# Fourier neural operator with a transformer block: spectra stored as (ky, kx, image), and one eviction of the spectral products moved to VectorE

## What is computed

```python
def _spectral_conv(h, w1, w2):
    xf = jnp.fft.rfft2(h)
    top = jnp.einsum('bixy,ioxy->boxy', xf[:, :, :M1, :M2], w1)
    bot = jnp.einsum('bixy,ioxy->boxy', xf[:, :, -M1:, :M2], w2)
    of = jnp.zeros(xf.shape, dtype=xf.dtype)
    of = of.at[:, :, :M1, :M2].set(top)
    of = of.at[:, :, -M1:, :M2].set(bot)
    return jnp.fft.irfft2(of, s=(h.shape[-2], h.shape[-1]))
for l in range(LAYERS):
    sc = _spectral_conv(h, w1r[l] + 1j * w1i[l], w2r[l] + 1j * w2i[l])
    pw = jnp.einsum('bihw,oi->bohw', h, pw_w[l]) + pw_b[l][None, :, None, None]
    y = sc + pw
    mean = y.mean(axis=(0, 2, 3), keepdims=True)
    var = y.var(axis=(0, 2, 3), keepdims=True)
    y = (y - mean) * jax.lax.rsqrt(var + EPS)
    y = y * gamma[l][None, :, None, None] + beta[l][None, :, None, None]
    h = jax.nn.gelu(y, approximate=False)
```

## Time and profile before

| | |
|---|---|
| Runs | 2538.08, 2528.74 and 2523.18 us, median 2528.74 |
| Profiled execution | 2528.25 us, of it the span 2526.5 us |
| Busy in the span | TensorE 2173.5 us (86%), VectorE 1648.5 (65%), ScalarE 1669.2 (66%), GpSimd 152.0 (6%) |
| Granted TensorE clock | 0.937 of full speed on average |
| HBM traffic | 203 GB/s over the span |
| Spectral products | four stages, of which layer 0's lies at 75.5 to 127.7 us and layer 1's at 532.5 to 584.9 us |

### The profile page before, as it was taken

How to read it: one execution, slowest core, us unless ns; L and a number is a source line. 1 busy time by engine, 2 the same in 40 slices (tenths; PEclk the granted TensorE clock), 3 DMA queues, 4 the chain that set the end, 5 groups by cost and what they waited for, 6 DMA issues and landing times. The chain is left out here.

```text
span 2526.5 us, 79368 instructions
## 1 busy us (share of the span) xinstructions
PE 2173.5 (86%) x34571; PEld 1449.5 (57%) x34571; DVE 1648.5 (65%) x2562; ACT 1669.2 (66%) x2640; POOL 152.0 (6%) x172
## 2 busy tenths in 40 slices
PE   6769979976997998599979967995999599964999
PEld 4657757765665776566657765664222355552444
DVE  3868878874777887577778874775000677754444
ACT  1924468876776887777778885675999466641333
POOL 0000000000000000000000000000000022202443
PEclk9989989988998999899989988998999699976999
DMA  5655567758997774899977659997652100012433
GB/s 184 227 169 203 185 255 260 240 177 274 343 349 283 265 262 151 276 329 331 323 269 257 217 201 302 360 370 274 218 178 88 37 2 2 2 29 55 105 87 71
DMA packets 174006, 518.62 MB, mean 205 GB/s; under 512 B 22687, under 2 KB 37759, under 8 KB 173439
## 3 DMA queue, kind: packets, MB, share of 16 engines
q1 hardware_dynamic: 173663, 513.55, 60.6%
HBM read 343.73 MB, written 170.37 MB: 203 GB/s over the span
## 5 line engine op out<-in xcount | busy, mean ns | idle before, releaser
L426 PE MATMUL P<-cst,mem 128*128 128x128 f32 (+1 forms) x3760 | 500.9, 282 | 54.2 <-DMA mem<-in_x 14.5
L426 PEld LDWEIGHTS P<-cst,mem 128*128 128x128 f32 (+1 forms) x3760 | 414.7, 143 | 162.2 <-issue 129.8
L685 ACT ACTIVATE mem<-P,small 128x512 f32<-128x512 f32 x512 | 310.6, 688 | 287.3 <-PE P L534 263.6
L844 DVE BATCH_NORM_STATS2 mem<-mem 128x6 f32<-128x512 f32 x512 | 315.2, 678 | 4.8 <-ACT mem L685 4.8
L882 DVE COPY mem<-P 128x512 f32<-128x512 f32 x384 | 247.9, 687 | 99.6 <-PE P L426 98.5
L534 PEld LDWEIGHTS P<-cst,mem 64*128 64x128 f32 (+1 forms) x5120 | 240.5, 166 | 100.7 <-issue 100.3
L534 PE MATMUL P<-cst,mem 64*128 64x128 f32 (+1 forms) x5120 | 262.6, 275 | 3.8 <-issue 3.5
L675 ACT ACTIVATE mem<-mem,small 128x1024 f32<-128x1024 f32 x192 | 229.2, 1250 | 49.7 <-DMA mem<-z_d 49.6
L837 DVE COPY mem<-P 128x512 f32<-128x512 f32 x256 | 165.0, 686 | 123.2 <-PE P L511 123.2
L832 DVE COPY mem<-P 128x512 f32<-128x512 f32 x256 | 165.3, 687 | 112.9 <-PE P L426 112.9
L719 ACT ACTIVATE mem<-mem,small 128x1024 f32<-128x1024 f32 x192 | 232.3, 1249 | 1.0
(11 more groups left out here) (164 smaller groups left out, 2941.1 us busy)
## 6 DMA issues: line engine op xcount, KB each, us to landing
mem<-z_d SPq DMA_DIRECT2D x348, 512.0 KB, 5.2
z_d<-mem SPq DMA_DIRECT2D x256, 512.0 KB, 6.2
mem<-in_wmix SPq DMA_DIRECT2D x64, 1024.0 KB, 8.6
G_d<-mem SPq DMA_DIRECT2D x128, 256.0 KB, 4.0
mem<-G_d SPq DMA_DIRECT2D x128, 256.0 KB, 7.6
hz<-z_d SPq DMA_DIRECT2D x64, 512.0 KB, 4.6
mdB<-dT_d SPq DMA_DIRECT2D x44, 384.0 KB, 5.6
mem<-in_x SPq DMA_DIRECT2D x128, 12.0 KB
```

The lines of the kernel that those rows point to most:

```text
L426: return nc.tensor.matmul(out, in_, ident[0:n, 0:n], start=True, stop=True, is_transpose=True)
L685: nc.scalar.activation(ychunk(l, a, h), P[4 + 2 * (a.q % 2) + h][:, :], ACT.Identity, bias=bias0 if first else pwb_c).then_inc(S["eY"], 1)
L844: nc.vector.bn_stats(so, ychunk(l, a, h)).then_inc(S["eS"], 1)
```

## The change

`XX` is stored as (ky, kx, image). The gathers of step s then read 1024 consecutive floats. All that write the spectra (L642, L795, L746 and L896; in the new file L644, L795, L746 and L902) write no two consecutive floats: the innermost loop goes over ky at 512 floats, 2 KB. The gathers keep their lines L812 and L813, and ScalarE's is now L658; ScalarE's one eviction is L664 there, and VectorE's L819. Mode 0 of all images becomes 32 consecutive floats. In `mix`, VectorE evicts the second bank of each step in place of ScalarE. Its loop is now ordered like ScalarE's: three gathers ahead, then for each step the eviction and the gather for step s+3.

```diff
--- before.py
+++ after.py
@@ -188,20 +188,22 @@
 
         def operands(s):
 
-            return SG[s % 3].rearrange("p (b k v i) -> p v b k i", b=2, k=16, v=2)
+            return SG[s % 3].rearrange("p (n v i) -> p v n i", v=2, i=IMG)
 
         def spectra(s):
 
-            return XX.rearrange("p (i k y) -> p y k i", k=16, y=KY)[:, 2 * s:2 * s + 2]
+            return XX[:, s * 1024:s * 1024 + 1024].rearrange("p (n i) -> p n i", i=IMG)
+
+        def image_modes(rows, image):
+            return XX.rearrange("p (y k i) -> p i k y", y=KY, k=16)[rows, image]
 
 
         def spectrum(r, image, q):
 
-            o = image * MODES + q * 256
-            return XX[r * 64:r * 64 + 64, o:o + 256].rearrange("p (i n) -> p i n", i=4)
+            return image_modes(slice(r * 64, r * 64 + 64), image)[:, q * 8:q * 8 + 8].rearrange("p (i j) y -> p i j y", j=2)
 
         def spectrum_bank(h, r):
-            return P[7][h * 64:h * 64 + 64, :].rearrange("p (i r n) -> p r i n", i=4, r=2)[:, r]
+            return P[7][h * 64:h * 64 + 64, :].rearrange("p (i r j y) -> p r i j y", i=4, r=2, j=2)[:, r]
 
 
         G_f = G_d.rearrange("i r k n -> (i r k n)")
@@ -638,8 +640,8 @@
             for b in range(PAIRS):
                 act.wait_ge(S["a0_mx"], b + 1)
                 for h in range(2):
-                    o, m = slice(h * 64, h * 64 + 64), (h * PAIRS + b) * MODES
-                    last = nc.scalar.activation(XX[0:64, m:m + MODES], P[2 * (b % 2)][o, :], ACT.Copy)
+                    o = slice(h * 64, h * 64 + 64)
+                    last = nc.scalar.activation(image_modes(slice(0, 64), h * PAIRS + b), P[2 * (b % 2)][o, :].rearrange("p (k y) -> p k y", k=16), ACT.Copy)
                 last.then_inc(S["a0_re"], 1)
             leave(act, "act")
 
@@ -660,8 +662,6 @@
                     act.wait_ge(S["pM"], l * 32 + 2 * s + 1)
                     wait(act, gst[s % 4], l * 128 + 32 * (s // 4) if s >= 4 else 0)
                     nc.scalar.activation(Gs[s % 4][:, 0:512], P[2 * s % 8][:, :], ACT.Copy).then_inc(S["eMd"], 1)
-                    act.wait_ge(S["pM"], l * 32 + 2 * s + 2)
-                    nc.scalar.activation(Gs[s % 4][:, 512:1024], P[(2 * s + 1) % 8][:, :], ACT.Copy).then_inc(S["eMa"], 1)
                     if s + 3 < MSTEPS:
                         stage(s + 3)
                 leave(act, "act")
@@ -791,11 +791,11 @@
             for b in range(PAIRS):
                 dve.wait_ge(S["a0_mx"], b + 1)
                 for h in range(2):
-                    o, m = slice(h * 64, h * 64 + 64), (h * PAIRS + b) * MODES
-                    last = nc.vector.tensor_scalar(XX[64:128, m:m + MODES], P[2 * (b % 2) + 1][o, :], -1.0, None, ALU.mult)
+                    o = slice(h * 64, h * 64 + 64)
+                    last = nc.vector.tensor_scalar(image_modes(slice(64, 128), h * PAIRS + b), P[2 * (b % 2) + 1][o, :].rearrange("p (k y) -> p k y", k=16), -1.0, None, ALU.mult)
                 last.then_inc(S["a0_im"], 1)
             dve.wait_ge(S["a0_re"], PAIRS)
-            dc = XX[0:64, :].rearrange("p (i m) -> p i m", m=MODES)[:, :, 0]
+            dc = XX[0:64, 0:IMG]
             link(nc.vector.tensor_scalar(dc, dc, fc0b4k[0:64, :], None, ALU.add))
             leave(dve, "dve")
 
@@ -811,8 +811,14 @@
                         dve.wait_ge(S["pM"], l * 32 + 2 * s - 4)
                     nc.vector.tensor_scalar(operands(s)[0:64, 1], spectra(s)[64:128], -1.0, None, ALU.mult).then_inc(S["sgD"], 1)
                     nc.vector.tensor_copy(operands(s)[:, 0], spectra(s)).then_inc(S["sgD"], 1)
+                for s in range(3):
+                    stage(s)
                 for s in range(MSTEPS):
-                    stage(s)
+                    dve.wait_ge(S["pM"], l * 32 + 2 * s + 2)
+                    wait(dve, gst[s % 4], l * 128 + 32 * (s // 4) if s >= 4 else 0)
+                    nc.vector.tensor_copy(Gs[s % 4][:, 512:1024], P[(2 * s + 1) % 8][:, :]).then_inc(S["eMa"], 1)
+                    if s + 3 < MSTEPS:
+                        stage(s + 3)
                 leave(dve, "dve")
 
             def inv(l, first):
```

## The result

| | before | changed |
|---|---|---|
| Runs, median | 2526.77 us (2523.18 to 2538.08, 5 runs) | 2549.67 us (2541.49 to 2553.36, 5 runs) |
| Ratio to before, 95% interval | | 1.007 (1.0043 to 1.0098) |
| Profiled execution | 2528.25 us, span 2526.5 | 2553.36 us, span 2551.6 |

What follows compares the result with a forecast made beforehand. ScalarE's queue was taken to bound the products and TensorE the forward stages; products -48.5, preamble +6.5, forward steady state +8 and end +12 gave -22 us from 2528.25, so 2506 us, range 2485 to 2530.

Steps and rivals of the forecast that it cites:

- The durations: Instruction times: gathers 0.69 us on VectorE, 1.06 on ScalarE; moved eviction 0.69; forward writers 617 and 594 ns.
- Rival 2: Products: VectorE's gathers stay at one element at a time, 1.22 us each, giving 2549 us; chance 0.1.
- rival 4: Spectra's writers: strided writes cost next to nothing, 26.5 us shrink to about 4, giving 2484 us; chance 0.08.
- The new stage, 37.4 us and "I add 2 us for three things": Layer 1's products: engines' sum 37.4 us, plus 2 for clock, DMA engines and SyncE's issuing queue, 39.4 us in all.
- Its term for the DMA engines: Layer 1's products: 12.6 MB of stores and loads at 407 GB/s take 31 us, fitting under 39 us.
- Rival 3: Products: DMA engines become the bound at 320 GB/s, 8 to 10 us more in layer 0, giving 2518 us; chance 0.1.
- The second dip of the clock: Products: a further lowering of TensorE's clock, one of three things covered together by 2 us.
- The parameter loads: Products: eight loads after step 6 hold SyncE's queue 6.0 us, delaying stores; 0.5 us counted, as operands are gathered ahead.
- The eviction moved to VectorE: Products: 0.69 us on VectorE against 0.60 on ScalarE; leaving it on ScalarE would cost some 1.5 us more a stage.
- The forward stages, +20: Layers 1 to 3: longer strided writes cost +8 us in steady state (0.2 a pair) and +12 at the stages' ends.
- Rival 1: Forward stages pay more: half a microsecond per pair instead of 0.2, and a longer tail, giving 2521 us; chance 0.2.
- The preamble: Layer 0's mixing: ScalarE's strided writes add 0.40 us to each of sixteen pairs, +6.5 us.

Runs made afterwards that it cites:

- half_stores: The changed kernel, but in layers 1 to 3 only half of the products' result rows are stored: 2520.43 us, 0.9979 of the kernel before.
- results_in_spectra: The changed kernel with the products' results written into the spectra's own columns, 16 buffers instead of 4: 2540.31 us, 1.0065 of the kernel before.
- params_first: The changed kernel with the eight parameter loads issued before step 0's stores instead of after step 6's: 2535.6 us, 1.0035 of the kernel before.
- layout_alone: The changed kernel with both evictions back on ScalarE, so only the layout is new: 2540.53 us, 1.0068 of the kernel before.

## Why the prediction was wrong

1. *The bound of the products before* (ScalarE's queue): right. With its gathers halved it is busy 26.4 of 47.0 us.
2. *The durations:* right throughout, within 4%. Rival 2, gathers at one element at a time, did not happen, nor did rival 4, cheap strided writes. Carrying the price of strided writes from 188 bytes to 2 KB was right.
3. *The new stage, 37.4 us and "I add 2 us for three things":* this step failed; layers 1 to 3 measured 47.0, 45.5 and 47.8 us. Its term for the DMA engines divided 12.6 MB by the 407 GB/s of one window and found 31 us, under the 39 of the engines. That window held loads and stores together. Stores alone go at 274 GB/s, and none can leave in the stage's first 6 us, so the traffic fills some 43 of the 45.5 us that the forecast leaves for it (an estimate, above), and the gap behind the parameter loads alone is more than the rest. half_stores shows that this traffic decides: with half the bytes the stage takes 41.0 to 41.7 us and the products, at 208.0, nearly the 206.6 that were forecast. Rival 3 named this and mis-sized it: it allowed 320 GB/s, for +12 us in all, where the loss was 26 us. A second term was put at nothing without a reason: TensorE's pace of 1.98 us a step was read between two pauses (the earlier trace rows show them, 0.41 and 1.01 us, `issue`), and twelve steps at 2.08 left them out. They take 6.6 to 11.2 us a stage, and results_in_spectra, where no eviction waits for a store, still needs 45.4 to 46.7 us. The second dip of the clock did come: from 569.3 to 573.0 us the granted clock was 0.63, and the two steps in it took 5.41 us instead of 3.94. How the loss divides between stores that are waited for and TensorE's pauses stays open, since both shrink with the traffic.
4. *The parameter loads:* foreseen in their place (step 11's evictions wait for step 7's store) and mis-sized at 0.5 us; they cost 2.5 to 3.9 us in each of layers 1 to 3 (params_first). I had argued that operands gathered ahead cover the wait. But from 573 to 578 us, in the gap, the DMA engines' share is 0.42 at 137 GB/s, and the stores that are held back come later.
5. *The eviction moved to VectorE:* priced rightly as an instruction (0.69 us), and worth nothing to the whole (layout_alone), where the sum had put about 1.5 us a stage on it.
6. *The forward stages, +20:* the mechanism was right, and the size of the steady state was not. I took 0.2 us per pair, from the one stall that I followed link by link; it was 0.65 (11.46 less 10.81), with a second stall behind ScalarE's late evictions. Rival 1 had priced 0.5 us and mentioned that path. Of the 12 us per stage VectorE's writer alone makes 7 and ScalarE's alone 3 to 5, by one run each.
7. *The preamble:* +5.1 measured for +6.5.

The two errors, 26 us on the products and 16 on the forward stages, lie on the same side, and with the +6.1 us elsewhere they turn a forecast of -22 into +25.

## What to carry to other kernels

When an engine's queue is the bound of a stage and is to be halved, add up what the stage moves by DMA, stores and loads apart, each at the rate of a window in which it runs alone, and ask when the first of it can start: one high figure of mixed traffic hides a slow kind. Add up too the pauses of the engine that is to set the pace next: they are in the trace before the change, where a slower engine hides them. A layout change moves a cost from readers to writers, and part of it shows wherever the writers sit beside a full TensorE (here 12 us of the 27 by which the writers' instructions of a stage grew); look for the layout that serves both, here two neighbours kept together, before trading one for the other. Where an engine is busy 30.0 of 30 us, every lengthened instruction on which it waits has to be followed for each of the engines, since the spare time of an engine's queue says nothing of when in the step it comes.

## What was not expected of the hardware

- Stores of results go at 274 and 278 GB/s with the DMA engines' busy share at 0.90 and 0.88, where weight loads mixed with them reach 401 to 413 GB/s at 1.03 to 1.04. Longer runs in memory (4 KB for 2) left the products where they were (220.2 against 219.4 us).
- Issues seem to wait for full DMA engines too (two stretches, no run made for it): the eight parameter loads, the largest 16 KB, held SyncE's queue for 6.0 us before, where the DMA engines' share was 0.85 in the first 3 us (561.4 to 564.4), and 8.2 us in the changed kernel, where it was 1.04 in the first 3.7 (569.3 to 573.0).
- TensorE pauses between pairs of the products' steps, 5.1 to 11.2 us a stage in layers 1 to 3, with nothing in the trace that it waits for; in results_in_spectra each of six pauses ends 1.2 to 1.5 us after a 16 KB transfer of the queue `instruction`.
- Two consecutive floats are enough for the writers: 420 ns (VectorE) and 391 ns (ScalarE) for 256 elements that jump 2 KB after each two, against 605 and 619 with a jump after each one, and 420 and 379 with none.
